# ScalarE issues six of the sixteen moves of n2's squares in every step of stage 2

## Time and profile before

| what | value |
|---|---|
| median of three runs | 736.8 us (736.57 to 742.76) |
| profiled execution | 736.94 us, of which the span of instructions is 735.2 us |
| TensorE busy (matmul) | 723.5 us, 98% of the span |
| VectorE / ScalarE / GpSimd busy | 537.9 / 372.4 / 122.9 us |
| mean granted TensorE clock | 0.997 of full speed |
| moves of n2's squares | 84 issued by SyncE's queue, 12 by ScalarE's |

### The profile page before, as it was taken

The page is one execution under the profiler, slowest core; times in us unless marked ns, Lnnn a source line. Parts: engine busy times, 40 slices in busy tenths (PEclk is TensorE's granted clock), DMA queues, the critical chain, the costliest instruction groups (busy, mean ns, idle before and its releaser), DMA issues. The chain is left out here.

```text
span 735.2 us, 10092 instructions
## 1 busy us (share of the span) xinstructions
PE 723.5 (98%) x3317; PEld 595.9 (81%) x3317; DVE 537.9 (73%) x808; ACT 372.4 (51%) x554; POOL 122.9 (17%) x220
## 2 busy tenths in 40 slices
PE   9999999999999999999999999999999989999998
PEld 8877888888888888888888888888887868788886
DVE  5798896695695596597587579876978576677584
ACT  4365446445536535635545542747558365564540
POOL 2000030031022004004004015105302112021110
PEclk9999999999999999999999999999999999999999
DMA  7949308926934952962970961642643616343322
GB/s 216 275 90 179 58 1 118 190 66 98 192 82 78 192 102 57 196 118 43 186 143 15 158 228 58 229 157 104 211 116 108 204 51 196 95 136 101 83 75 86
DMA packets 119311, 93.54 MB, mean 127 GB/s; under 512 B 75584, under 2 KB 103263, under 8 KB 117231
## 3 DMA queue, kind: packets, MB, share of 16 engines
q1 hardware_dynamic: 116174, 88.13, 50.6%
q10 hardware_dynamic: 2912, 5.01, 2.1%
q0 software_dynamic: 192, 0.00, 0.1%
HBM read 32.28 MB, written 25.20 MB: 78 GB/s over the span
## 5 line engine op out<-in xcount | busy, mean ns | idle before, releaser
L688 PE MATMUL pc<-x_h,wg_h 128*128 128x512 f32 x224 | 87.5, 391 | 1.2 <-DVE s_l L1770 1.2
L690 PE MATMUL pc<-x_h,wg_l 128*128 128x512 f32 x224 | 87.2, 389 | 0.0
L689 PE MATMUL pc<-x_l,wg_h 128*128 128x512 f32 x224 | 87.2, 389 | 0.0
L1569 DVE TENSOR_TENSOR_SCAN stage_b<-alpha,carry,stage_b 128x512 f32<-128x512 f32 x64 | 78.5, 1268 | 0.0
L688 PEld LDWEIGHTS pc<-x_h,wg_h 128*128 128x128 f32 x224 | 42.1, 188 | 11.6 <-issue 1.7
L806 PE MATMUL pm<-t_h,wt_h 128*128 128x512 f32 x128 | 50.2, 392 | 0.8 <-DVE t_l L1582 0.6
L1201 ACT ACTIVATE ctx_t<-ctx_t,col_all 128x512 f32<-128x512 f32 x32 | 23.2, 724 | 54.0 <-DVE ctx_t L1549 54.0
L688 PE MATMUL pm<-wo_h,s_h 128*128 128x512 f32 x128 | 50.0, 390 | 0.0
L808 PE MATMUL pm<-t_h,wt_l 128*128 128x512 f32 x128 | 49.9, 390 | 0.0
L807 PE MATMUL pm<-t_l,wt_h 128*128 128x512 f32 x128 | 49.9, 390 | 0.0
L690 PE MATMUL pm<-wo_h,s_l 128*128 128x512 f32 x128 | 49.8, 389 | 0.0
(11 more groups left out here) (280 smaller groups left out, 1883.5 us busy)
## 6 DMA issues: line engine op xcount, KB each, us to landing
x_planes<-x_pairs SPq DMA_DIRECT2D x56, 256.0 KB, 6.9
xt_scratch<-x_t SPq DMA_DIRECT2D x8, 1024.0 KB, 10.0
n_scratch<-stage_a SPq DMA_DIRECT2D x8, 1024.0 KB, 9.5
ctx_t<-xt_scratch SPq DMA_DIRECT2D x16, 512.0 KB, 6.9
x_pairs<-n_scratch SPq DMA_DIRECT2D x14, 512.0 KB, 5.6
out_dram<-x_tok SPq DMA_DIRECT2D x28, 256.0 KB, 2.3
x_planes<-stage_b SPq DMA_DIRECT2D x84, 64.0 KB, 2.0
mod<-mod_scratch ACTq DMA_DIRECT2D x8, 512.0 KB, 3.7
```

The lines of the kernel that those rows point to most:

```text
L688: nc.tensor.matmul(acc, ah, bh, start=start and q == 0, stop=False)
L689: nc.tensor.matmul(acc, ah, bl, start=False, stop=False)
L690: last = nc.tensor.matmul(acc, al, bh, start=False, stop=stop and q == n - 1)
L1569: nc.vector.tensor_tensor_scan(tr[:, m % 2, :], alpha[:, 1 + d:2 + d].to_broadcast([P, BLK]), tr[:, m % 2, :], carry[:, D - d, m:m + 1], A ...
```

## The change

ScalarE's list of six moves is now used in all six steps that move squares. In steps 2 and 7 nothing changes: three ahead of relu and three behind it in step 2, all six ahead of relu in step 7. In steps 3 to 6 ScalarE issues the six behind `relu_part` and ahead of `scale_n2`, and SyncE issues the other ten.

```diff
-        def shares_moves(j):
-            return j == 1 or j == LAST - 1
...
                 for q in range(4):
                     for a in range(4):
-                        if not (shares_moves(j) and (q, a) in BY_ACT):
+                        if (q, a) not in BY_ACT:
                             move_square(sp, q, a)
...
-                if shares_moves(i - 1):
-                    move_shares(i - 1, BY_ACT[:3])
-                if i == LAST:
-                    move_shares(i - 1, BY_ACT[3:])
+                before = {2: 3, LAST: len(BY_ACT)}.get(i, 0)
+                if before:
+                    move_shares(i - 1, BY_ACT[:before])
                 relu_part(i)
-                if i == 2:
-                    move_shares(1, BY_ACT[3:])
+                if i < LAST:
+                    move_shares(i - 1, BY_ACT[before:])
                 for m in range(NC):
                     scale_n2(i - 1, m)
```

## The result

The changed kernel takes 731.47 us (median of four runs, 731.42 to 732.72) against 736.75 us for the kernel before on the same chip: a ratio of 0.9939, with an interval of 0.9911 to 0.9966. The profiled execution took 731.42 us with a span of 729.6 us, and its mean granted clock was 1.0. The forecast was 731.2.

A forecast was written before the change was run, and what follows sets the result against it. TensorE's matmuls fill 98% of the span, so only its waits could be won, the main one set by SyncE issuing sixteen DMAs. 736.94 - 4.74 - 0.97 = 731.2 us; range 730.0 to 735.5.

The forecast's parts named there:

- the third l1_product of step 4 waited: Sign of being wrong: TensorE waiting ahead of the third l1_product in step 4, 5 or 6.
- R + 9.2: Latest harmless start of scale_n2 in step 3, counted in us from relu's end, R; a later start was a sign of being wrong.
- The bound: TensorE's long wait in step 4: its chain 3.19 us late, headed by SyncE's queue issuing sixteen DMAs in step 3.
- The rival of bytes: Moves limited by their bytes, not their issue, so sharing between two queues gains nothing: 736.9 us, chance 4%.
- SyncE's ten moves, about 6.5 us: Steps 3 to 6: ten issues instead of sixteen take 6.42 us, not 10.91, so step 3's store goes 4.5 us sooner.
- Output tile 2 at 576.2: Step 3: with the store issued at about 573.9, VectorE's output tile 2 can run at 576.2.
- the 4.74 us go whole: Ahead of step 4's third l1_product: 3.33 us of wait plus 1.41 us of slow matmuls all vanish.
- The clock's 1.41 us: Step 4: slow matmuls at granted clock 0.50 after TensorE's long wait, 1.41 us, go with that wait.
- Step 5's 0.97 us: Step 5: TensorE's wait for an output tile, 0.97 us, goes because the store is issued sooner.
- `scale_n2` costs nothing, bounds R + 4.6 to R + 8.5: Last move lands within these bounds after relu's end, R, inside limits R + 9.2 (step 3) and R + 10.0 (step 4).
- the rival of late moves: ScalarE's six moves land partly late beside the loads, R + 10.5 in step 3: 733.0 us, up to 736, chance 17%.
- The sum: Whole kernel: 736.94 - 4.74 - 0.97 = 731.2 us, 0.8% less.

The follow-up runs named there:

- e2: Changed kernel, but in steps 3 to 6 SyncE's store of output tile 0 waits until all sixteen moves have landed: 737.65 us.
- e1: Kernel before, no sharing in steps 3 to 6, with the store of output tile 0 between SyncE's tenth and eleventh moves: 730.23 us.
- e7: Changed kernel with step 2's six ScalarE moves ahead of relu and the store of output tile 0 behind SyncE's eighth move in steps 3 to 6: 728.9 us.
- e10: Kernel before, store of output tile 0 between SyncE's tenth and eleventh moves in steps 3 to 6, step 2's six ScalarE moves ahead of relu: 729.2 us.
- e9: Changed kernel, but in steps 3 to 5 SyncE issues its four loads only when all sixteen moves have landed: 730.6 us.
- e6: Changed kernel, but in steps 3 to 6 the store of output tile 0 stands behind the eighth of SyncE's ten moves: 730.62 us.
- e4: Changed kernel, but ScalarE shares the moves in steps 4 to 6 and not in step 3 (steps 2 and 7 as always): 735.29 us.
- e3: Changed kernel, but of steps 3 to 6 only step 3 shares the moves (steps 2 and 7 as always): 732.93 us.
- e5: Changed kernel, but in step 2 all six of ScalarE's moves go ahead of relu instead of three: 729.74 us.
- e11: Changed kernel, but in steps 3 to 6 ScalarE issues its six moves ahead of relu: 730.38 us.

## Why the prediction was right, and where it was not

The time and the head of the chain were right. Still, two of the signs that the prediction named for being wrong came: the third l1_product of step 4 waited (0.76 us lost), and `scale_n2` of step 4 started at R + 9.83, past R + 9.2.

- **The bound.** Right: issue time on SyncE's queue ahead of one store was the head of the chain. The same store held back takes everything away again (e2), and brought forward without sharing it gives everything (e1).
- **The rival of bytes, and the rule quoted with it.** Refuted for the queue as it was ordered: issuing from two queues won 736.75 - 731.47 = 5.3 us. The Trainium skill (DMA: Bandwidth & Descriptors, section "Issuing engines are not separate DMA queues") calls the issue cost usually small relative to the DMA; here sixteen issues took 10.91 us where one move lands in 2.0 to 2.1 us, and the measurement decides. Where the store no longer stands behind all the issues the sentence of the Trainium skill fits: e7 and e10, with two queues and with one, are 0.3 us apart. The Trainium skill says in the same section that DMAs of all issuing engines run on the same sixteen engines; e9 agrees with it, as ScalarE's moves land some 4 us sooner without SyncE's loads beside them.
- **SyncE's ten moves, about 6.5 us.** Right in step 3, 6.41; in steps 4 to 6 they took 7.44, 7.18 and 6.83.
- **Output tile 2 at 576.2, "the 4.74 us go whole".** This is the term that was mis-sized. I took the store's landing from before, 2.3 us, where ScalarE issued nothing beside it. Now its issue alone took 2.20 us and the landing 4.23. Tile 2 came at 577.66, `x3_sum_part` 1.0 us later than forecast, and 0.76 us of the wait stayed; e6 shows that it was the store. That ScalarE's moves stand beside it explains at most a part (2.8 and 3.3 us in steps 4 and 5); what made the rest is open.
- **The clock's 1.41 us.** They went, since the clock behind the place was 1.00. But I priced them as if they followed from the wait. They do not always: the clock fell to 0.51 behind 2.70 us lost in e2, and stayed at 1.00 behind 3.50 us lost in e4. The term belongs in the sum only for most executions. In e4 the executions with a mean clock of 1.0 and the others have medians of 733.5 and 735.8 us, 2.3 apart, more than the 1.41 of the term; what makes the rest is not shown. Nor are kernels without a long wait free of it: one of six executions had a mean clock of 0.997 in e1 (734.14 us) and of 0.998 in e6 (734.93 us), and no trace shows what stood ahead of it there.
- **Step 5's 0.97 us.** Right, gone.
- **`scale_n2` costs nothing, bounds R + 4.6 to R + 8.5.** Right in the sum, wrong in the bound: step 4 had R + 9.83, and the margin that I put at 1.5 us was 0.2. Step 5's low part of x2 ended at 618.04, with TensorE due at 618.19. I had the upper bound from step 2, with three moves beside the loads; here six stand there. The limits held: R + 9.2 in step 3 was enough in e1, and R + 10.72 in e3 cost a wait. Whether the last move goes out well ahead of the loads or just ahead of them hangs on one long issue (e3), so the rival of late moves, at 17%, was nearer than the time shows.
- **The sum.** 731.2 against 731.4 in the profiled execution is closer than its terms, and that is luck: 0.76 us too much was taken off, and 0.57 us came from elsewhere, 0.39 of it from ahead of anything the change touches.

## What to carry to other kernels

When an engine waits for a small DMA, look first at what stands ahead of that DMA on its own queue and count issues, not bytes: moving one store past six issues did as much as a second queue did. When transfers are handed to a second queue, say what else runs in the window in which they will land, and take their landing from a row with as many of them in that company. Place them where the queue is empty, even ahead of work that seems urgent, if that work has idle time in front of it (relu in e5), or if nobody needs its result so soon (relu in e11, which came 1.2 to 2.3 us late without a wait on TensorE).

## What the runs showed of the hardware

An issue of a move takes 0.60 us as a rule (the median of the stage in every trace), but some issues, of moves, stores and loads, take 1.1 to 2.3. The long ones mostly stand beside packets of another DMA queue, q8, of the kind "instruction"; q14 has such packets too. Here the store's issue of step 3 in the changed kernel, and the queues of the same stretch (packets, MB, share of 16 engines):

```profile
573.34 2.20 SPq L476 DMA_DIRECT2D out_dram<-x_tok  x1
```
```profile
q8 instruction: 1, 0.02, 4.2%
q14 instruction: 1, 0.01, 1.4%
```

Two issues that stand side by side on the two queues, SyncE's 2.20 us from 573.34 and ScalarE's 1.61 us from 573.95, are long together, and such packets pass at 573.46 and 574.67. The kernel before has it too (an issue of 1.25 us at 573.80 and a packet at 573.60). It returns in all thirteen traces: behind 538 us they have 37 issues of a move with 1.1 us or more, and each of them overlaps a packet of q8. Five long issues of a store, one of them of 1.21 us at 605.80 in the changed kernel, overlap none. What causes it was not tried.
